# A graph layer's segment sum: the weighting matrix held stationary, groups of 896 edges

## The reference: what is computed

```
def gcn_layer(x, W, b):
    support = x @ W                                   # [12500, 256] @ [256, 256]
    msgs = support[edge_src] * edge_weight[:, None]   # 200000 rows
    return segment_sum(msgs, edge_dst) + b
h = elu(gcn_layer(layernorm(x), W1, b1))
h = elu(gcn_layer(h, W2, b2))
x = x + h
xf = layernorm(x)                                     # then a routed FFN
H = gelu(xf @ ffn_W1 + ffn_b1)                        # 256 -> 1024
probs = softmax(H @ Wg + bg);  e = argmax(probs)      # 8 experts, one per node
x = x + probs[e] * (H @ Wd[e] + bd[e])
```

## Time and profile before

| what | value |
|---|---|
| median of three timed runs | 4539.37 us |
| span of the profiled execution (the page gives no other time for it) | 5639.2 us |
| PE / PEld busy | 3611.2 / 3303.4 us |
| DVE / ACT / POOL busy | 2125.6 / 1218.9 / 3287.1 us |
| mean granted TensorE clock | 0.741 |
| gathers of edge rows: raw x, normalised x, h | 268, 1296, 1564 |

### The profile page before, as it was taken

The page is one execution under the profiler, slowest core; times in us unless marked ns, Lnnn a source line. Parts: engine busy times, 40 slices in busy tenths (PEclk is TensorE's granted clock), DMA queues, the critical chain, the costliest instruction groups (busy, mean ns, idle before and its releaser), DMA issues.

```text
span 5639.2 us, 84567 instructions
## 1 busy us (share of the span) xinstructions
PE 3611.2 (64%) x21407; PEld 3303.4 (59%) x21408; DVE 2125.6 (38%) x7215; ACT 1218.9 (22%) x2041; POOL 3287.1 (58%) x3464
## 2 busy tenths in 40 slices
PE   4555445555555545557667676666776776678998
PEld 3554444555544545456666666666666666667777
DVE  6663233223232322224334443333443433354332
ACT  4551110000000000013223232232232322232111
POOL 5666556666666666655565655555555555524555
PEclk6666666666666666668777777778777777789999
DMA  4543323333333333323333333333333333344444
GB/s 149 166 154 92 90 86 91 95 96 93 96 95 96 94 96 93 94 77 103 104 115 113 114 114 114 106 108 111 113 112 110 111 111 104 107 130 142 156 156 138
DMA packets 248031, 626.81 MB, mean 111 GB/s; under 512 B 66279, under 2 KB 113014, under 8 KB 247358
## 3 DMA queue, kind: packets, MB, share of 16 engines
q0 software_dynamic: 173664, 491.88, 30.3%
q1 hardware_dynamic: 69646, 103.75, 5.1%
q10 hardware_dynamic: 4176, 26.61, 1.3%
HBM read 519.22 MB, written 103.73 MB: 110 GB/s over the span
## 4 chain that ended last, share of the span: by engine, by line
PE 40%; issue 24%; another core or an unknown queue 4%; DVEq 4%; DVE 3%; DMA 2%; ACT 1%; POOL 0%; POOLq 0%; ACTq 0%; SPq 0%
PE pA L1381 18%; PE pB L1422 13%; PE pZ L1391 3%; PE pC L1404 3%; DMA aggT<-pay_scratch,ids 2%; PE pA L1536 1%; DVE S L927 1%; DVEq L927 1%; PE pZ L1415 1%; DVEq L953 1%; PE pT L1410 0%; DVE aggT L978 0%; PE pC L1526 0%; DVEq L978 0%
## 5 line engine op out<-in xcount | busy, mean ns | idle before, releaser
L1381 PE MATMUL pA<-S,rows 128*128 128x96 f32 x12544 | 1857.1, 312 | 961.7 <-issue 639.8
L1381 PEld LDWEIGHTS pA<-S,rows 128*128 128x128 f32 x12544 | 1797.0, 228 | 1039.1 <-issue 1033.8
L549 POOL DMA_INDIRECT rows<-h_scratch,idx x1564 | 1491.4, 954 | 1107.8 <-issue 424.2
L549 POOL DMA_INDIRECT rows<-xn_scratch,idx x1296 | 1227.9, 947 | 742.7 <-issue 366.2
L1422 PE MATMUL pB<-work,w 128*128 128x128 f32 x3232 | 776.5, 380 | 707.3 <-issue 702.3
L1422 PEld LDWEIGHTS pB<-work,w 128*128 128x128 f32 x3232 | 656.0, 279 | 818.9 <-issue 818.2
L927 DVE TENSOR_SCALAR S<-iota_p,tdst,twgt 128x96 f32<-128x96 f32 x3168 | 852.8, 351 | 288.2 <-issue 280.7
L978 DVE TENSOR_TENSOR aggT<-aggT,pA 128x192 f32 x784 | 278.0, 355 | 1340.3 <-remote 851.1
L1030 DVE TENSOR_TENSOR zb<-pZ,brow 128x256 f32<-128x256 f32 x198 | 84.0, 424 | 1150.0 <-issue 692.8
L1391 PE MATMUL pZ<-wg,stage 128*128 128x256 f32 x784 | 276.0, 485 | 213.0 <-ACT stage L642 126.2
L1536 PE MATMUL pA<-aggT,work 128*128 x1680 | 387.5, 384 | 10.8 <-DVE work L1311 10.1
(11 more groups left out here) (200 smaller groups left out, 2613.9 us busy)
## 6 DMA issues: line engine op xcount, KB each, us to landing
pay_scratch<-work SPq DMA_DIRECT2D x98, 512.0 KB
rows<-h_scratch,idx POOLq DMA_INDIRECT x1564
rows<-xn_scratch,idx POOLq DMA_INDIRECT x1296
work<-in_x_dram ACTq DMA_DIRECT2D x15, 896.0 KB
xn_scratch<-work ACTq DMA_DIRECT2D x14, 896.0 KB
h_scratch<-work SPq DMA_DIRECT2D x98, 128.0 KB
pay_scratch<-work SPq DMA_DIRECT2D x98, 128.0 KB
work<-in_x_dram SPq DMA_DIRECT2D x97, 128.0 KB
```

Of the source, the lines that this page charges most:

```text
L549: pool.indirect_dma_start(rows[:, s, t, :], None, source, bass.IndirectOffsetOnAxis(at, 0))\
L1381: last = mm(to[:, k * W:(k + 1) * W], rows[:, slot, t, k * P:(k + 1) * P], Sx[:, t, :], start=(t == 0), stop=(t == T - 1))
```

## The change

T is 7 (groups of 896 edges), SLOTS 4, HALF 2, W 128. That gives 224 groups and NH = 112 halves of 14 gathers. S becomes the stationary operand and the gathered rows the moving one, 256 columns wide. The sum now arrives with nodes on the partitions; ACT copies the sums of a half (two groups, 512 columns) from PSUM to `gsum`, PE transposes it in four 128x128 pieces, and DVE adds it from PSUM into `aggT`. The S matrices of the next half are built before the tick; their scalars are copied ahead to a small table `tnext`. Ticks are allowed at 0.875 per half (PACE). Raw rows are normalised one group at a time. The order on ACT in a raw half changes: the chunk's work comes behind the second group.

```diff
-    T = 4
+    T = 7
-    W = 96
-    SLOTS = 8
+    W = P
+    SLOTS = 4
+    PACE = 0.875
...
+            def copy_sums(layer, h):
+                act.wait_ge(s_mm[layer], HALF * h + HALF + SLOTS)
+                act.activation(gsum[:, :], pG2, ACT.Copy).then_inc(s_gc[layer], 1)
...
@@ ACT, raw_half
-                row_root(2 * h + 2, ahead)
-                row_normalise(2 * h + 2, ahead)
+                row_root(HALF * h + 2, ahead)
+                row_normalise(HALF * h + 2, ahead)
+                copy_sums(0, h)
+                row_root(HALF * h + 3, ahead + 1)
+                row_normalise(HALF * h + 3, ahead + 1)
                 if with_chunk:
                     chunk_normalise(h, half)
                     chunk_store(h, half)
                     chunk_root(h + 1)
-                row_root(2 * h + 3, ahead + 2)
-                row_normalise(2 * h + 3, ahead + 2)
...
@@ ACT, loop over the other halves of both layers
                    for half in range(2):
                         h = 2 * i + half
+                        copy_sums(layer, h)
                         _, start, end = half_flags(act, layer, h)
                         ticks(act, start, end, lambda j: (tick1, tick2)[layer](j, h))
...
@@ DVE
+            def copy_columns(layer, h, buf):
+                v.tensor_copy(tnext[:, buf, :, :, :], tab[:, :, :, bass.ds(h * HALF, HALF)]).then_inc(s_tab[layer], 1)
+            def group_matrices(layer, h, u, buf):
+                dve.wait_ge(s_mm[layer], HALF * h + u + (SLOTS - HALF + 1))
                 for t in range(T):
+                    last = v.tensor_scalar(S[:, u, t, :], iota_w[:, :], tnext[:, buf, 0, t, u:u + 1],
+                                           tnext[:, buf, 1, t, u:u + 1], ALU.is_equal, ALU.mult)
+            def add_groups(layer, h):
+                bases = bases_of(h)
+                dve.wait_ge(s_tr[layer], h + 1)
+                for u in range(HALF):
+                    hold(dve, s_add[layer], HALF * h + u + HALF)
+                    to = aggT[:, :, bass.ds(bases[u], W)]
+                    v.tensor_tensor(to, to, pSUM[:, u * C:(u + 1) * C].rearrange("p (k n) -> p k n", k=KC), ALU.add)
...
@@ DVE, raw_half
+                        for u in range(HALF):
+                            row_statistics(HALF * h + HALF + u, ahead + u, value)
+                            group_matrices(0, h + 1, u, 1 - half)
+                            row_scales(HALF * h + HALF + u, ahead + u)
+                        if with_chunk:
+                            chunk_statistics(h + 1, 1 - half)
+                        add_groups(0, h)
                         if with_chunk:
                             chunk_scales(h + 1)
+                        copy_columns(0, h + 2, half)
...
@@ DVE, all other halves
+                        build_S(layer, h + 1, 1 - half)
                         ticks(dve, start, end, (tick1, tick2)[layer])
-                        for u in range(0, HALF, 2):
-                            bases = pair_ready(layer, h, u)
-                            for n in range(2):
-                                add_group(layer, h, u + n, bases[n])
-                            next_matrices(layer, h, u)
+                        add_groups(layer, h)
+                        copy_columns(layer, h + 2, half)
...
@@ PE
+            def group_products(slot, u):
+                for t in range(T):
+                    last = mm(pG2[:, u * C:(u + 1) * C], S[:, u, t, :], rows[:, slot, t, :],
+                              start=(t == 0), stop=(t == T - 1))
+                return last
+            def transpose_sums(layer, h):
+                pe.wait_ge(s_gc[layer], h + 1)
+                pe.wait_ge(s_add[layer], HALF * h + HALF)
+                for u in range(HALF):
+                    for k in range(KC):
+                        at = u * C + k * P
+                        last = nc.tensor.transpose(pSUM[:, at:at + P], gsum[:, at:at + P], ident[:, :])
+                last.then_inc(s_tr[layer], 1)
...
                     pe.wait_ge(s_S[layer], g + 1)
-                    if u % 2 == 0:
-                        pe.wait_ge(s_add[layer], g + 2)
-                    products(half * HALF + u, S[:, u, :, :], group_sum(u), s_mm[layer])
+                    group_products(half * HALF + u, u).then_inc(s_mm[layer], 1)
                 if not raw:
                     ticks(pe, start, end, tick)
+                transpose_sums(layer, h)
```

More of the change, by code:

```diff
@@ L291, in bass_gnn_then_routed_ffn @@
         s_mm = [sem(f"group_multiplied_{l}") for l in range(2)]
+        s_gc = [sem(f"group_sums_copied_{l}") for l in range(2)]
+        s_tr = [sem(f"group_sums_transposed_{l}") for l in range(2)]
+        s_tab = [sem(f"table_columns_copied_{l}") for l in range(2)]
         s_add = [sem(f"group_added_{l}") for l in range(2)]
@@ L694, in load_chunk, with row_root, row_normalise @@
                 act.dma_start(xc[buf], x[chunk_rows(c), :].rearrange("(p t) f -> p t f", t=LNT)).then_inc(s_xin, 16)
[L696 to L701, removed]
-                for n in range(2):
[L703 to L706, removed]
+            def row_root(g, s):
+                act.wait_ge(s_var, g + 1)
+                act.activation(std[:, s, :], mv[:, s, :, 1], ACT.Sqrt, bias=epsc[:, :]).then_inc(s_std, 1)
+            def row_normalise(g, s):
+                act.wait_ge(s_nmr, g + 1)
+                for t in range(T):
+                    last = act.activation(rows[:, s, t, :], rows[:, s, t, :], ACT.Identity,
+                                          bias=nmr[:, s, t:t + 1], scale=rstd[:, s, t:t + 1])
+                last.then_inc(s_na, 1)
             def chunk_root(c):
@@ L866, in _ @@
             LO4 = LOr[:, 0:NG].rearrange("o (h g) -> o h g", g=HALF)
-            for r in range(2):
+            for r in range(HALF // 2):
                 pair = regs[0:1, 0:NH, 1 + r]
@@ L981, in next_matrices @@
-            def next_matrices(layer, h, u):
-                for n in range(2):
-                    build_S(layer, HALF * h + HALF + u + n, u + n)
-            def row_statistics(pair, s, value):
-                for n in range(2):
-                    dve.wait_ge(s_gath[0][s + n], value - 16 * FEWER[s + n])
-                    for t in range(T):
-                        last = v.bn_stats(stats[:, s + n, t, :], rows[:, s + n, t, :])
+                bases = bases_of(h)
+                for u in range(HALF):
+                    overflow(layer, HALF * h + u, bases[u])
@@ new lines, in add_groups, with row_statistics @@
+            def add_groups(layer, h):
+                bases = bases_of(h)
+                dve.wait_ge(s_tr[layer], h + 1)
+                for u in range(HALF):
+                    hold(dve, s_add[layer], HALF * h + u + HALF)
+                    to = aggT[:, :, bass.ds(bases[u], W)]
+                    v.tensor_tensor(to, to, pSUM[:, u * C:(u + 1) * C].rearrange("p (k n) -> p k n", k=KC), ALU.add)\
+                     .then_inc(s_add[layer], 1)
+            def row_statistics(g, s, value):
+                dve.wait_ge(s_gath[0][s], value - 16 * FEWER[s])
+                for t in range(T):
+                    last = v.bn_stats(stats[:, s, t, :], rows[:, s, t, :])
```

141 lines of the change are left out of this document (58 added, 83 removed).

## The result

The changed kernel takes 4699.23 us (median of 5 runs, 4691.27 to 4704.31), the kernel before 4542.18 us in the same series (5 runs, 4538.06 to 4546.99). The ratio is 1.0348, 95% interval [1.0337, 1.0359]: slower by 157 us. Predicted were 4655 us, range 4525 to 4800, own range of case A 4590 to 4740.

What follows compares the result with a forecast made beforehand. The prediction held the kernel bound by POOL's issue of gathers at 1.25 us each. Raw stretch 35, second layer 75 and layer ends 5 summed to +115 us on 4539, forecast 4655 us, range 4525 to 4800.

Steps and rivals of the forecast that it cites:

- case A: Whole kernel: raw stretch and second layer both leave POOL's pace, forecast 4655 us, range 4590 to 4740; chance 0.45.
- What bounds the kernel before: Both layers: timed runs are bound by the issue of gathers on POOL, 1.25 us each, with hardly a pause.
- slow stretches: PE and DVE start one instruction every 0.7 us for some 10 us per half, mainly in the profiled execution.
- 4604 us floor: Whole kernel before: start, two layers of gathers at 1.25 us, change of layers and a 648.4 us tail sum to 4604.
- Case D: Whole kernel: faster, if timed runs have POOL pauses that fewer PE instructions shorten; -100 us, 4440; chance 0.15.
- Products: PE's matmuls of 256 columns step at 0.216 us, 6.05 us a half; instructions halve, PE's time doesn't.
- Second layer: Products, S and tick form one chain, 19.1 us per half with a tick: +75 us, bounds 0 and +280.
- products to pC: Second layer, PE's wait from products' end to tick: signals 0.3, seven S 1.95, DVE 1.02 us.
- clock: Second layer: PE's lull before the tick drops its granted clock to half, +2.2 us a half, bounds 0 and 4.
- Raw stretch: First layer, 14 halves with a chunk: DVE's `chunk_scales` waits for ACT, 19.9 us a half; +35 us, bounds 0 and +55.
- Wider S beside the gathers: Both layers: S of 128 columns on DVE doesn't slow the gathers, 0; the skill's port rule would give 109 us.
- Ends of the layers: End of both layers: longer last group, plus copy and transposes, 2.5 us twice, +5 us.

Runs made afterwards that it cites:

- e5: Changed kernel with raw-stretch chunk put back between the two groups and second-layer tick put back before S on DVE: 4590.84 us, ratio 1.0112.
- e1: Changed kernel with DVE doing the tick before building the next half's S, second layer only: 5995.09 us, ratio 1.064.
- e2: Changed kernel with the chunk of x between the two groups on ACT and DVE, raw stretch only: 6061.86 us, ratio 1.0756.
- c1: The changed kernel run again unedited as control: 4700.89 us, ratio 1.0363.
- e4b: Changed kernel with 12 unread filler matmuls on PE behind each second-layer half's products, second of three such runs: 6319.39 us, ratio 1.1211.

## Why the prediction was right, point by point

**What bounds the kernel before: right.** The 4540.9 us of the first table row and e5's second layer, which returns to within 1% of the pace, agree with it. The reason that I gave for the slow stretches was wrong: "belong mainly to the profiled execution". In three of four series the timed runs took 5630 us as well. They are a condition in which the program runs or doesn't; that the shown median was free of them was right, and the sum stood on that. My 4604 us floor was 60 too high, since the profiled execution's tail was 648 us instead of the 590 of the changed kernel's traces.

**Case D (faster, 0.15): fell.** By the first table row the timed runs had no pauses to win, and the gathers' undisturbed step is 1.25 us in the traces of both conditions. Nor does the change win in the other condition, where I would have looked for it: with the first layer of e1 and the second of e2, the rest from e2, the changed kernel would take about 24 + 2383 + 32 + 2993 + 657 = 6089 us beside 5631, some 460 slower (estimated from these traces, since c1 didn't meet it).

**Products: right.** They step at 0.216 us per record of 256 columns, 6.21 us per 28 (predicted 6.05).

**Second layer, +75 predicted, +87 to +109 measured: the mis-sized term.** That 75 is so near is in part luck. It lies between +57, against the gathers' pace, and +95, against a layer of 1922 us that I got by taking the tail as 648.4. With a tail of 590 the layer of the timed runs is 1954 us, and my own parts give +57. Those parts, over halves with a tick: products to pC predicted 3.3 us, measured 2.85 in one half of a turn and 5.9 in the other, mean 4.4; clock predicted +2.2, measured +1.6 to +1.8; S of 128 columns 0.256 us each, predicted 0.275; halves without a tick 9.7, predicted 10.5. The half with a tick came to 19.6 to 19.8 against 19.1. So the wait was sized too small and the clock too large. What I missed is DVE's halt at the turn of its loop. It was there before the change too: in the trace of before, DVE stands 4.0 us behind the last record of 43 of 49 turns of the second layer, and 1.6 us again at the next branch. There DVE went from the turn into the tick, while PE still had its products to do. The edit that took this cover away I counted only by the one group that must wait. That the order of S and tick makes the pauses of the second layer is shown (e5: 75 us fall to 2). That the halt is what lifts every second half from 18 to about 22 us is read from the trace, where the halves that begin with a turn are the long ones. Its price in total wasn't measured.

**Raw stretch, +35 predicted, +44 to +45 measured.** The sum gave 19.9 us a half, the trace 20.4. `chunk_scales` does wait for ACT behind the chunk. Timeline of ACT, POOL and DVE, changed kernel:

```profile
174.41 3.53 ACT L724 ACTIVATE work<-work,LG 128x256 f32<-128x256 f32 x7
...
178.45 0.95 POOL L554 DMA_INDIRECT rows<-in_x_dram,idx  x1 [5.31 <-PE pA L1383]
178.51 0.30 ACT L719 ACTIVATE LG<-LG,epsc 128x7 f32<-128x7 f32 x1 [0.56 <-ACT work L724]
178.84 0.20 DVE L1027 RECIPROCAL LG<-LG 128x7 f32<-128x7 f32 x1 [3.66 <-ACT LG L719]
```

But only 18 of them go when that order is undone (e5): the larger part, 26 us, is not the wait on ACT that I named. e5 keeps it with groups of seven tiles, four slots and S of 128 columns; which of these it is stays open. Between 120 and 270 us of e5 all pauses of POOL are released by PE, whose granted clock is 0.68 in the mean there, so PE's clock is a candidate as well, and no run tests it. I had the size nearly and the cause in part.

**Wider S beside the gathers, 0 predicted: nearly.** In the earlier trace rows nothing was to be seen; over whole layers it is about 11 us (e5's table of steps). The rule of the Trainium skill ("SBUF — State Buffer", section "SBUF: two separate sides") had the sign right. The 109 us that I worked out by it are ten times too much. Half of that is S itself, which grew from 0.24 to 0.257 us and not to 0.275; the other half is that a step with three or more S in it grew by 0.014 to 0.019 us, and not by what each S had grown. One stretch of 8 steps was too little to price 0.01 us a step on.

**Ends of the layers +5:** they can't be told apart in the traces. The start took 3 us more where I took 0.

**Chances.** A came true, with 157 us against 115. What lies between is 12 to 34 us of the second layer, 14 of the first and 3 of the start. The halt of DVE and the part of the raw stretch that e5 keeps are what I did not see; the first is not priced by itself.

## What to carry to other kernels

An operation put ahead of another on an engine with time to spare lends its wait to everything behind it. Before moving it, add what that engine's sequencer does at the turn of its loop: no row of instructions shows it, and only idle time with "<-issue" betrays it. When the bound is a steady issue of gathers, compare the mean of the chain per unit with the pace and the slots between; here 1 to 2 us over 17.5 in a half was nearly all of the loss. And run the kernel before in each series: a condition that changes it from 4540 to 5630 us makes every absolute expectation void, while a layer that an edit doesn't touch stays a control.

## What the runs showed of the hardware

The slow condition is worth knowing. In it PE and DVE nearly stop some time into an unbroken series of gathers and, in the two places shown (e4b above, e2 here), resume 3.4 and 4.7 us behind the start of its last one. Timeline of e2, second layer, POOL, ACT and DVE; the gather is the last of 21 without a pause:

```profile
3055.03 0.95 POOL L554 DMA_INDIRECT rows<-h_scratch,idx  x1 [0.30 <-issue]
3059.70 0.60 ACT L646 ACTIVATE gsum<-pA 128x512 f32<-128x512 f32 x1 [24.93 <-remote]
3059.70 1.88 DVE L939 TENSOR_SCALAR S<-iota_p,tnext 128x128 f32<-128x128 f32 x7 [11.21 <-remote]
```

Two engines start in the same instant on PE's products, whose own last record ended at 3040.9, 18.8 us before. The packets of the gathers took the same time in both conditions (0.157 us the mean in the changed kernel's trace, 0.155 in e2's), those of the instruction queue too (0.40 and 0.41). It was there in three series on three chips and absent in one on one of these chips. What brings it about, and whether it is instructions or signals that come late, no run here settles.

At the turn of the second layer's loop DVE stood 3.2 us and again 1.7 us at the next branch (2.8 and 1.6 in e2, in the other condition), with one 8 KB packet of instructions in each halt. In the first layer's shorter loop it stood 0.25 us and fetched nothing. The clock lost in a lull of 7 us (1.00 to 0.50) was back at 1.00 6 us into the tick (from 3024 on); it was lost in the lull of 2.84 us too, behind which 12 pC matmuls took 2.83 us instead of 1.66, at a granted clock of 0.58 in the mean (3037 to 3040). Fillers in the lull kept it.
